# First attention of a four-stage block on one core: query items of one head by 512 tokens, values for two groups at once, masks written into the score bank, one block with its opening

## The chip, the cores and the metric

One NeuronCore of a Trainium2 chip runs the whole program. The metric is device time in microseconds (us) of one execution. TensorE (PE) multiplies, VectorE (DVE), ScalarE (ACT) and GpSimd (POOL) do everything between, SyncE's queue (SP) issues transfers.

## What is computed

`x` has 8 sequences of 128 tokens with 512 features. Four stages follow each other, each `x = x + tanh(gate) * stage(layernorm(x))`. Only the first changes:

```python
q = (query @ Wq).reshape(nb, q_len, H, D).transpose(0, 2, 1, 3)      # 32 heads of 128
k = (key @ Wk).reshape(nb, q_len, KVH, D).transpose(0, 2, 1, 3)      # 8 key heads
v = (value @ Wv).reshape(nb, q_len, KVH, D).transpose(0, 2, 1, 3)
q = q * cos + _rotate_half(q) * sin
k = k * cos + _rotate_half(k) * sin
k = jnp.repeat(k, GROUPS, axis=1)                                    # 4 query heads share a key head
v = jnp.repeat(v, GROUPS, axis=1)
scores = jnp.einsum('bhqd,bhkd->bhqk', q, k) / jnp.sqrt(jnp.float32(D))
scores = jnp.where(mask == 0, jnp.float32(-1000000000.0), scores)
attn = jax.nn.softmax(scores, axis=-1)
x = jnp.einsum('bhqk,bhkd->bhqd', attn, v)
return x.transpose(0, 2, 1, 3).reshape(nb, q_len, H * D) @ Wo
```

Keys and values come from `ctx`, queries from the normalised `x`. After it come a dequantised feed-forward, a second attention and a mixture of experts, which the change leaves as they are.

## The kernel before

Every large product is done in three fp32r parts: `product` (lines 119 to 124) multiplies the held operand's high part by the streaming operand's high part (L122) and low part (L123), and its low part by the streaming high part (L124). So each operand needs a copy to fp32r by ACT (`_hi`) and a subtraction by DVE or POOL (`_lo`).

**Opening** (its own `nc.Block`, lines 197 to 300). SP loads positions, gates, `x` in two halves, weights of group 0, the turned context and the mask. DVE makes layernorm statistics and normalises; PE turns the eight tiles (`norm_turn`, L116); ACT and DVE make `xT_hi` and `xT_lo` (L108, L98). POOL issues eight gathers of rotary rows (L219) first of all its work and then subtracts weights; PE turns the rotary rows (L293); ACT copies the context to `cT_hi` (L251), DVE and POOL each make two of the four `cT_lo`. At the end PE projects two items (`FIRST_ON_PE`).

**Attention** (a second block). Eight groups `g`, one key head and four query heads each. A group has eight units `u`, one sequence each, and ten items, each a 128x512 result in a bank: an item goes PE `project`, DVE `item_products` (one product with cos, L516, two with sin, L519), POOL `item_sum` (L410; for keys L406 and a scaling L408). A query item is two heads by 256 tokens: 24 products of 256 columns (`project_queries`, L170). A key item is 12 products of 512 columns. `place_of` says where an item goes; items 10 and up belong to the next group.

A unit goes through PE `score` (L634), DVE `keep_scores` (four `copy_predicated` of the open scores from the bank into `filled`, L528, and a maximum over `filled`, L531), ACT `exps` (L454), DVE `invert`, POOL `normalise` (L414), PE `turn_probs` (L641), ACT `probs_upper` (L461), DVE `probs_rest` (L539), PE `attend` (3 products), ACT `out_upper`, DVE `out_rest`, PE `project_out` (12 products), DVE `add_out` (L548).

The order of each engine is written out by hand: in step `s` of a group PE does `score(s)`, the step's items, in steps 0 and 1 half of the values, then `attend(s-2)`, `project_out(s-3)`, `turn_probs(s-1)`. So units run in a pipeline four steps deep. The values of a group are made turned (weights held, context streaming, two halves of 12 products), copied by ACT (`keep_values`), turned by PE (`turn_values`, L624), then split.

Weights of the next group are prepared inside the group: ACT does `queries_upper` in steps 4 and 5, `keys_values_upper` at the end of step 3, behind `probs_upper` of the step, and `out_weights` (four copies, L448) at the end of step 2. POOL follows with `wk_lo` (L152), `wv_lo`, `wq_lo`, `wo_lo` (L397). Items by step:

```python
ITEMS_OF_STEP = [[5], [6], [7], [8], [9], [10], [11], [12, 13, 14]]
FIRST_ITEMS = [0, 1, 2, 3, 4]
```

Items 2 and 3 (12 and 13 for the next group) are the key items, so keys of the next group are first needed in step 7. `score` of an even unit waits for the item sums that it reads (`rope_sum`).

## Time and profile before

| | us |
|---|---|
| median of 3 timed runs | 943.28 (940.91 to 947.6) |
| the profiled execution's own time | 939.19 |
| its span, first to last instruction | 937.3 |
| mean granted TensorE clock | 0.965 |
| busy: PE, PE weight loads, DVE, ACT, POOL | 849.8, 732.2, 665.1, 407.6, 427.7 |

The profile is one execution. Its page gives busy time by engine, 40 slices of the span, the chain of work that ended last, and the costliest groups of instructions. The trace behind it gives each instruction's start and duration (us from the span's start). A product's printed duration contains its fill and drain, which overlap with its neighbours: what a product costs in a stream is the distance from its start to the next start.

### The profile page before, as it was taken

How to read it: one execution, taken by the hardware profiler on the slowest of the kernel's cores; microseconds unless marked ns; L12 is line 12 of the kernel's file. 1: busy time of each engine (PE TensorE's matmuls, PEld its weight loads, DVE VectorE, ACT ScalarE, POOL GpSimd, SP SyncE). 2: the span in 40 equal slices, each digit the busy share in tenths (PEclk: the TensorE clock that was granted, in tenths of full speed). 3: DMA queues.
4: the chain of work that ended last, by engine and by line, in shares of the span. 5: the costliest groups of instructions: out<-in, count | busy, mean ns of one | idle time of the engine just before them, and what ended most of it. 6: DMA issues, size and time to landing. Idle time of an engine off the chain costs nothing. (4 is left out here: it accounts for less than half of the span.)

```text
span 937.3 us, 14384 instructions
## 1 busy us (share of the span) xinstructions
PE 849.8 (91%) x4952; PEld 732.2 (78%) x4952; DVE 665.1 (71%) x1332; ACT 407.6 (43%) x1001; POOL 427.7 (46%) x341
## 2 busy tenths in 40 slices
PE   2799999999999999999999999987899887999990
PEld 1788889889889888988988988865778665777770
DVE  5767758767767767766776776747582677999874
ACT  3335235335324424424424433435313425978870
POOL 6548417436435534633642732506300007877830
PEclk9999999999999999999999999998999967999995
DMA  8201101101101100200300200007100545999817
GB/s 345 84 1 45 68 2 46 68 0 45 67 0 45 67 0 7 105 0 0 112 0 0 90 1 1 1 1 287 45 5 8 224 180 177 348 339 346 324 40 270
DMA packets 23048, 88.88 MB, mean 95 GB/s; under 512 B 6512, under 2 KB 7024, under 8 KB 15200
## 3 DMA queue, kind: packets, MB, share of 16 engines
q1 hardware_dynamic: 16864, 78.90, 22.8%
q0 software_dynamic: 6144, 9.46, 2.9%
q8 instruction: 23, 0.38, 0.2%
q14 instruction: 17, 0.14, 0.0%
HBM read 85.18 MB, written 13.63 MB: 105 GB/s over the span
## 5 line engine op out<-in xcount | busy, mean ns | idle before, releaser
L410 POOL TENSOR_TENSOR qT<-straight,turned 128x512 f32<-128x512 f32 x64 | 82.5, 1288 | 239.6 <-DVE turned L519 239.6
L454 ACT ACTIVATE probs<-filled,negmax 128x128 f32<-128x128 f32 x256 | 99.7, 391 | 126.9 <-DVE negmax L531 126.9
L122 PE MATMUL bank<-xT_hi,wq_hi 128*128 128x256 f32 x512 | 149.3, 292 | 0.0
L124 PE MATMUL bank<-xT_hi,wq_lo 128*128 128x256 f32 x512 | 144.7, 283 | 0.0
L123 PE MATMUL bank<-xT_lo,wq_hi 128*128 128x256 f32 x512 | 144.6, 282 | 0.0
L519 DVE TENSOR_TENSOR turned<-bank,sinT 64x512 f32<-64x512 f32 x160 | 110.1, 688 | 2.2
L122 PE MATMUL bank<-wo_hi,oT_hi 128*128 128x512 f32 x256 | 102.4, 400 | 5.3 <-DVE oT_lo L543 4.2
L124 PE MATMUL bank<-wo_hi,oT_lo 128*128 128x512 f32 x256 | 100.1, 391 | 0.0
L123 PE MATMUL bank<-wo_lo,oT_hi 128*128 128x512 f32 x256 | 99.9, 390 | 0.0
L122 PEld LDWEIGHTS bank<-xT_hi,wq_hi 128*128 128x128 f32 x512 | 97.1, 190 | 0.4
L123 PEld LDWEIGHTS bank<-xT_lo,wq_hi 128*128 128x128 f32 x512 | 97.0, 189 | 0.3
L516 DVE TENSOR_TENSOR straight<-bank,cosT 128x512 f32<-128x512 f32 x80 | 55.3, 691 | 58.4 <-PE bank L124 57.0
L124 PEld LDWEIGHTS bank<-xT_hi,wq_lo 128*128 128x128 f32 x512 | 96.7, 189 | 0.0
L461 ACT ACTIVATE pT_hi<-bank 128x512 fp32r<-128x512 f32 x64 | 38.1, 595 | 115.1 <-PE bank L641 115.1
L548 DVE SCALAR_TENSOR_TENSOR x<-bank,gates,x 128x512 f32<-128x512 f32 x64 | 47.9, 748 | 36.8 <-PE bank L124 36.8
L1345 DVE TENSOR_TENSOR cT_lo<-ring,cT_hi 128x1024 fp32r<-128x1024 f32 x56 | 68.1, 1221 | 7.9 <-ACT cT_hi L1058 7.9
L414 POOL TENSOR_TENSOR probs<-probs,invtotal 128x512 f32<-128x512 f32 x64 | 66.6, 1041 | 12.7 <-DVE invtotal L535 12.7
L634 PE MATMUL bank<-kT,qT 128*128 128x128 f32 x512 | 67.6, 275 | 0.0
L122 PE MATMUL bank<-cT_hi,xT_hi 128*128 128x512 f32 x144 | 60.8, 422 | 5.6 <-DVE xT_lo L1339 5.5
L543 DVE TENSOR_TENSOR oT_lo<-bank,oT_hi 128x512 fp32r<-128x512 f32 x64 | 44.2, 691 | 29.2 <-ACT oT_hi L466 28.1
L122 PEld LDWEIGHTS bank<-wo_hi,oT_hi 128*128 128x128 f32 x256 | 48.0, 188 | 19.7 <-DVE oT_lo L543 5.4
L634 PEld LDWEIGHTS bank<-kT,qT 128*128 128x128 f32 x512 | 62.3, 192 | 0.1
(218 smaller groups left out, 2051.3 us busy)
## 6 DMA issues: line engine op xcount, KB each, us to landing
ring<-in_ew SPq DMA_DIRECT2D x28, 1024.0 KB, 6.9
raw_big<-in_wq SPq DMA_DIRECT2D x8, 1024.0 KB
raw_big<-in_wo SPq DMA_DIRECT2D x8, 1024.0 KB
early_w<-in_ew SPq DMA_DIRECT2D x8, 1024.0 KB
ring<-picked SPq DMA_DIRECT2D x8, 512.0 KB, 7.1
x<-in_x SPq DMA_DIRECT2D x2, 1024.0 KB
raw_k<-in_wk SPq DMA_DIRECT2D x8, 256.0 KB
raw_v<-in_wv SPq DMA_DIRECT2D x8, 256.0 KB
```

Of the source, the lines that this page charges most:

```text
L122: nc.tensor.matmul(out_, hi, r_hi, start=start, stop=False)
L123: nc.tensor.matmul(out_, hi, r_lo, start=False, stop=False)
L124: return nc.tensor.matmul(out_, lo, r_hi, start=False, stop=stop)
L410: nc.gpsimd.tensor_tensor(dst, shaped(straight[:, k, :], key), shaped(turned[:, k, :], key), ALU.add).then_inc(rope_sum, 1)
L414: nc.gpsimd.tensor_tensor(probs[:, u % 2, :, :], probs[:, u % 2, :, :], invtotal[:, u % UNITS, :].unsqueeze(2).broadcast_to([P, GR, S]), A ...
L454: ex = nc.scalar.activation(probs[:, u % 2, h, :], filled[:, u % UNITS, h, :], ACT.Exp, bias=negmax[:, u % UNITS, h:h + 1], accum_out=tota ...
L516: nc.vector.tensor_tensor(shaped(straight[:, k, :], key), shaped(bank[:, :], key), spread_over(cosT[:, tok], key), ALU.mult)
L519: last = nc.vector.tensor_tensor(shaped(turned[dst, k, :], key), shaped(bank[src, :], key), spread_over(sinT[src, tok], key), ALU.mult)
L543: nc.vector.tensor_tensor(oT_lo[:, u % 2, :, :], bank_o[:, :].rearrange("p (h t) -> p h t", h=GR), oT_hi[:, u % 2, :, :].bitcast(F32), ALU ...
L548: nc.vector.scalar_tensor_tensor(x[:, u % UNITS, :], bank_y[:, :], gates[:, 0:1], x[:, u % UNITS, :], ALU.mult, ALU.add).then_inc(y_added, 1)
L634: mm = nc.tensor.matmul(bank_scores[u % 2][:, h * S:(h + 1) * S], qT[:, (u // 2) % 2, h, q], kT[:, keys], start=True, stop=True)
L1345: nc.vector.tensor_tensor(expert_lo(k)[:, rows, :], ring[k % RING][:, rows, :], expert_hi(k)[:, rows, :].bitcast(F32), ALU.subtract).then_ ...
```

## The change

- Both blocks become one, `filled` and `vT` go, and the opening's buffers lie over attention buffers that are used later (`over`). The layernorm buffer has four tiles.
- A query item is one head by 512 tokens: 12 products of 512 columns. Items are reordered: 0 is keys of the first 512 tokens, 1 to 4 are heads for them, 5 keys of the rest, 6 to 9 heads for them. Steps 3 and 7 hold two items, all others one. `score` waits for sums at units 0 and 4 alone.
- Values are made unturned (context held, weights of two groups streaming, 256 columns): four fills of 24 products for a pair of groups. Groups 0 and 1 are filled in the opening; groups 2, 4 and 6 fill for themselves and the next in steps 0, 1, 2 and 4. `keep_values` and `turn_values` go.
- `keep_scores` writes -1e9 into the score bank where a key is closed; the maximum and the exponentials read the bank; `score(u)` waits for the exponentials of unit `u-2`.
- Weight copies and remainders for queries are done by head (four of 512 columns), for keys at the end of step 3, for values only in odd groups (steps 3 and 6).
- Opening: POOL does the key remainder before its gathers, and two value remainders between the fifth and the sixth gather; DVE makes all four `cT_lo`; ACT interleaves tiles 4 to 7 with the four context copies and does the value copies behind them; PE turns half of the rotary rows, makes item 0, turns the other half, then values and items 1 to 4 in turns.

The core of the diff:

```diff
+        def ln_bank(n, t):
+            return psum[t % 2 if n else 4 + t % 2]
...
+            ctx_raw = over("wo_hi", "ctx_raw", [P, KC, T])
+            xn = over("qT", "xn0", [P, 4, E], skip=4 * GR * HALF)
+            rotary = over("pT_hi", "rotary", [P, NB, 2 * D])
+            mask_raw = over("oT_hi", "mask_raw", [P, NB, S], I32)
+            raw_v1 = over("oT_lo", "raw_v1", [P, KC, D])
...
+            ITEMS_OF_STEP = [[5], [6], [7], [8, 9], [10], [11], [12], [13, 14]]
+            FIRST_ITEMS = [0, 1, 2, 3, 4]
+            KEY_ITEMS = (0, 5)
+            FILLS = NB // 2
+            FILL_OF_STEP = {0: 0, 1: 1, 2: 2, 4: 3}
...
+            def fills(g, odd):
+                return not odd and (not isinstance(g, int) or 0 < g < KVH)
+            def place_of(item):
+                i = item % ITEMS
+                if i in KEY_ITEMS:
+                    half = KEY_ITEMS.index(i)
+                    tok = slice(half * HALF, (half + 1) * HALF)
+                    return kT[:, tok], tok, True
+                half, h = (0, i - 1) if i < 5 else (1, i - 6)
+                return qT[:, half, h, :], slice(half * HALF, (half + 1) * HALF), False
+            def head_of(item):
+                return (item % ITEMS - 1) % 5
...
+                    load_out(0)
                     sp.dma_start(loaded[:, :, :], a["wk1"]).then_inc(g_in[0], 16)
-                    sp.wait_ge(wq_lo_s, 2)
-                    sp.dma_start(raw_big[:, :], a["wo"][0]).then_inc(big_in, 16)
+                    with sp.Fori(1, KVH - 2, 2) as g:
+                        load_keys(g)
+                        load_queries(g)
+                        load_out(g)
+                        load_values(g + 1)
+                        load_keys(g + 1)
+                        load_queries(g + 1)
+                        load_values(g + 2)
+                        load_out(g + 1)
+                    load_keys(KVH - 1)
+                    load_queries(KVH - 1)
+                    load_out(KVH - 1)
...
+                    def keys_rest(g):
+                        wait(pool, wk_hi_s, g, 1, 1)
+                        nc.gpsimd.tensor_tensor(wk_lo[:, :, :], raw_k[:, :, :], wk_hi[:, :, :].bitcast(F32), ALU.subtract).then_inc(wk_lo_s, 1)
+                    def values_weight_rest(g, half, raw):
+                        cols = slice(half * D, (half + 1) * D)
+                        wait(pool, wv_hi_s, g, 1, 1)
+                        nc.gpsimd.tensor_tensor(wv_lo[:, :, cols], raw[:, :, :], wv_hi[:, :, cols].bitcast(F32), ALU.subtract).then_inc(wv_lo_s, 1)
...
+                    def group(g, odd):
+                        for step, u, items, _, _, _ in steps(g):
+                            if step in (4, 5) and more(g):
+                                queries_rest(g + 1, 2 * (step - 4))
+                                queries_rest(g + 1, 2 * (step - 4) + 1)
+                            if u is not None and not items:
+                                normalise(g, u)
+                            for item in items:
+                                item_sum(g, item)
+                                if item == items[0]:
+                                    normalise(g, u)
+                            if step == 2 and u is not None:
+                                out_weights(g)
+                            if step == 3 and more(g):
+                                keys_rest(g + 1)
+                                if odd:
+                                    values_weight_rest(g + 1, 0, raw_v)
+                            if step == 6 and more(g) and odd:
+                                values_weight_rest(g + 2, 1, raw_v)
+                    nc.gpsimd.memset(masked[:, :], MASKED)
                     nc.gpsimd.memset(key_scale[:, :], float(D) ** -0.5)
+                    keys_rest(0)
                     pool.wait_ge(pos_step, 3)
                     for t in TILES:
                         pool.indirect_dma_start(
                             out=rotary[:, t, :], out_offset=None, in_=a["rotary"],
                             in_offset=bass.IndirectOffsetOnAxis(ap=pos_row[:, t:t + 1], axis=0)).then_inc(in_rot, 16)
-                    keys_values_rest(pool, 0)
-                    queries_rest(pool, 0, 0)
-                    queries_rest(pool, 0, 1)
-                    for c in (1, 3):
-                        pool.wait_ge(ctx_hi, c + 1)
-                        nc.gpsimd.tensor_tensor(cT_lo[:, c, :], ctx_raw[:, c, :], cT_hi[:, c, :].bitcast(F32),
-                                                ALU.subtract)
+                        if t == 4:
+                            values_weight_rest(0, 0, raw_v)
+                            values_weight_rest(1, 1, raw_v1)
+                    for h in range(GR):
+                        queries_rest(0, h)
+                    for item in FIRST_ITEMS:
+                        item_sum(0, item)
+                    group(0, False)
+                    with pool.Fori(1, KVH - 2, 2) as g:
+                        group(g, True)
+                        group(g + 1, False)
+                    group(KVH - 1, True)
+                    group(KVH, False)
...
+                    def keys_upper(g):
+                        wait(act, k_in, g, 16, 16)
+                        wait(act, proj_mm, g, ITEMS, 6 - ITEMS)
+                        nc.scalar.activation(wk_hi[:, :, :], raw_k[:, :, :], ACT.Copy).then_inc(wk_hi_s, 1)
...
+                    def exps(g, u):
+                        wait(act, score_max, g, UNITS, u + 1)
+                        wait(act, pT_mm, g, UNITS, u - 1)
+                        for h in range(GR):
+                            ex = nc.scalar.activation(probs[:, u % 2, h, :], bank_scores[u % 2][:, h * S:(h + 1) * S], ACT.Exp,
+                                                      bias=negmax[:, u % UNITS, h:h + 1], accum_out=total[:, u % UNITS, h:h + 1])
...
+                    def group(g, odd):
+                        for step, u, items, turn, attend, _ in steps(g):
+                            if step in (4, 5) and more(g):
+                                if step == 4:
+                                    wait(act, proj_mm, g, ITEMS, 10)
+                                queries_upper(g + 1, 2 * (step - 4))
+                                queries_upper(g + 1, 2 * (step - 4) + 1)
+                            if u is not None:
+                                exps(g, u)
+                            if attend is not None:
+                                out_upper(g, attend)
+                            if step in FILL_OF_STEP and fills(g, odd):
+                                values_upper(g, FILL_OF_STEP[step])
+                            if turn is not None:
+                                probs_upper(g, turn)
+                            if step == 2 and u is not None:
+                                out_weights(g)
+                            if step == 3 and more(g):
+                                keys_upper(g + 1)
+                                if odd:
+                                    wait(act, v_mm, g, 2, 2)
...
                     nc.scalar.activation(gates[:, :], gates_raw[:, :], ACT.Tanh)
                     norm_sqrt(act, 0, HALVES[0])
-                    norm_upper(act, 0, 0)
-                    norm_upper(act, 0, 1)
-                    keys_values_upper(act, 0)
-                    norm_upper(act, 0, 2)
-                    norm_upper(act, 0, 3)
+                    for t in HALVES[0]:
+                        norm_upper(act, 0, t)
+                    keys_upper(0)
                     norm_sqrt(act, 1, HALVES[1])
-                    queries_upper(act, 0, 0)
-                    queries_upper(act, 0, 1)
-                    for t in HALVES[1]:
-                        norm_upper(act, 0, t)
                     for c in range(KC):
-                        act.wait_ge(in_ctx[c // 2], 16)
+                        norm_upper(act, 0, 4 + c)
+                        act.wait_ge(in_ctx[c], 16)
                         nc.scalar.activation(cT_hi[:, c, :], ctx_raw[:, c, :], ACT.Copy).then_inc(ctx_hi, 1)
-                    keep_cos(0)
-                    keep_cos(1)
+                    act.wait_ge(v_in, 32)
+                    values_weight_upper(0, 0, raw_v)
+                    values_weight_upper(1, 1, raw_v1)
+                    keep_rotary(0)
+                    for h in range(GR):
+                        queries_upper(0, h)
+                    keep_rotary(1)
+                    for f in range(FILLS):
+                        values_upper(0, f)
+                    act.wait_ge(ctx_lo, KC)
+                    group(0, False)
...
+                    def keep_scores(g, u):
+                        wait(dve, score_mm, g, UNITS, u + 1)
+                        nc.vector.memset(gatepost[:, :], 0.0)
+                        for h in range(GR):
+                            kept_ = nc.vector.copy_predicated(bank_scores[u % 2][:, h * S:(h + 1) * S], closed_key[:, u, :],
+                                                              masked[:, :].broadcast_to([P, S]))
+                        kept_.then_inc(score_kept, 1)
+                        wait(dve, score_kept, g, UNITS, u + 1)
+                        nc.vector.tensor_reduce(negmax[:, u, :], bank_scores[u % 2][:, :].rearrange("p (h k) -> p h k", h=GR),
+                                                AX.X, ALU.max, negate=True).then_inc(score_max, 1)
...
+                            if step in FILL_OF_STEP and fills(g, odd):
+                                values_rest(g, FILL_OF_STEP[step])
...
+                    def make_values(g, f):
+                        wait(pe, wv_lo_s, g, 1, 2)
+                        wait(pe, v_lo_s, g, 2, f)
+                        for j in range(2):
+                            tok = slice((2 * f + j) * S, (2 * f + j + 1) * S)
                             for c in range(KC):
-                                mm = product(bank[:, :], wk_hi[:, c, :], wk_lo[:, c, :], cT_hi[:, c, tok], cT_lo[:, c, tok], c == 0, c == KC - 1)
-                        else:
-                            mm = project_queries(j, bank, tok)
-                        mm.then_inc(proj_mm, 1)
...
                     def score(g, u):
-                        if u % 2 == 0:
-                            wait(pe, rope_sum, g, ITEMS, 4 + u if u else 3)
-                        wait(pe, score_kept, g, UNITS, u - 1)
+                        if u % 4 == 0:
+                            wait(pe, rope_sum, g, ITEMS, 5 + 5 * (u // 4))
+                        wait(pe, exp_done, g, UNITS, u - 1)
                         keys = slice(u * S, (u + 1) * S)
-                        q = slice((u % 2) * S, (u % 2 + 1) * S)
+                        q = slice((u % 4) * S, (u % 4 + 1) * S)
                         for h in range(GR):
-                            mm = nc.tensor.matmul(bank_scores[u % 2][:, h * S:(h + 1) * S], qT[:, (u // 2) % 2, h, q], kT[:, keys], start=True, stop=True)
...
+                    def attend(g, odd, u):
+                        own = odd if u >= 0 else not odd
+                        if not own and u % 2 == 0:
+                            wait(pe, v_lo_s, g, 2, u // 2 + 1)
                         wait(pe, pT_lo_s, g, UNITS, u + 1)
                         wait(pe, o_lo_s, g, UNITS, u)
-                        product(bank_o[:, :], v_hi[:, u % UNITS, :], v_lo[:, u % UNITS, :], pT_hi[:, u % 2, :], pT_lo[:, u % 2, :], True, True).then_inc(o_mm, 1)
+                        cols = slice(D, 2 * D) if own else slice(0, D)
+                        product(bank_o[:, :], v_hi[:, u % UNITS, cols], v_lo[:, u % UNITS, cols], pT_hi[:, u % 2, :], pT_lo[:, u % 2, :], True, True).then_inc(o_mm, 1)
...
+                    turn_rotary(0)
+                    pe.wait_ge(wk_lo_s, 1)
+                    for c in range(KC):
+                        pe.wait_ge(ctx_lo, c + 1)
+                        mm = product(bank_rope[0][:, :], wk_hi[:, c, :], wk_lo[:, c, :], cT_hi[:, c, 0:HALF], cT_lo[:, c, 0:HALF], c == 0, c == KC - 1)
+                    mm.then_inc(proj_mm, 1)
+                    turn_rotary(1)
+                    make_values(0, 0)
+                    pe.wait_ge(ln_lo, NB)
+                    for item in FIRST_ITEMS[1:]:
+                        project(0, item)
+                        if item < FILLS:
+                            make_values(0, item)
+                    group(0, False)
+                    with pe.Fori(1, KVH - 2, 2) as g:
+                        group(g, True)
+                        group(g + 1, False)
```

## Rows read from the trace of the kernel before

**Rows 1.** Windows: length; busy of PE, PEld, DVE, ACT, POOL; PEclk; DMA; GB/s
```profile
190.18:263.51 73.33, 73.33 (x466) 65.36 (x465) 52.34 (x113) 29.54 (x92) 35.18 (x28) 1.00 0.10 36
49.08:116.85 67.77, 64.56 (x420) 56.93 (x419) 48.88 (x108) 26.92 (x88) 38.20 (x31) 1.00 0.11 40
782.60:786.60 4.00, 4.00 (x10) 3.15 (x11) 2.33 (x3) 2.65 (x4) 3.13 (x3) 0.50 0.37 129
```
**Rows 2.** Timeline of PE: scores that open steps of a group, start and us
```profile
200.59 1.06 PE L634 MATMUL bank<-kT,qT 128*128 128x128 f32 x8
...
212.14 1.06 PE L634 MATMUL bank<-kT,qT 128*128 128x128 f32 x8
...
219.75 1.06 PE L634 MATMUL bank<-kT,qT 128*128 128x128 f32 x8
...
227.49 1.06 PE L634 MATMUL bank<-kT,qT 128*128 128x128 f32 x8
```
**Rows 3.** Timeline of PE in step 7: where pieces of work begin
```profile
253.98 0.40 PE L122 MATMUL bank<-cT_hi,wk_hi 128*128 128x512 f32 x1
...
256.77 0.28 PE L122 MATMUL bank<-xT_hi,wq_hi 128*128 128x256 f32 x1
...
259.63 0.40 PE L122 MATMUL bank<-pT_hi,v_hi 128*128 128x512 f32 x1
260.33 0.39 PE L122 MATMUL bank<-wo_hi,oT_hi 128*128 128x512 f32 x1
...
263.08 0.60 PE L641 MATMUL bank<-ident,probs 128*128 128x128 f32 x4
263.51 1.06 PE L634 MATMUL bank<-kT,qT 128*128 128x128 f32 x8
```
**Rows 4.** Timeline of ACT, then POOL, behind step 3
```profile
227.69 0.60 ACT L461 ACTIVATE pT_hi<-bank 128x512 fp32r<-128x512 f32 x1 [2.70 <-PE bank L641]
228.18 0.62 ACT L163 ACTIVATE wk_hi<-raw_k 128x512 fp32r<-128x512 f32 x1
...
229.40 1.29 POOL L152 TENSOR_TENSOR wk_lo<-raw_k,wk_hi 128x512 fp32r<-128x512 f32 x1 [0.97 <-ACT wv_hi L164]
```
**Rows 5.** Timeline of the opening
```profile
13.91 0.95 POOL L219 DMA_INDIRECT rotary<-in_rotary,pos_row  x1 [0.30 <-issue]
...
16.70 0.60 ACT L108 ACTIVATE xT_hi<-bank 128x512 fp32r<-128x512 f32 x1 [0.46 <-PE bank L116]
...
23.12 0.60 ACT L108 ACTIVATE xT_hi<-bank 128x512 fp32r<-128x512 f32 x1
...
28.34 3.62 PE L293 MATMUL bank<-ident,rotary 128*128 128x128 f32 x16
...
29.08 1.05 ACT L251 ACTIVATE cT_hi<-ctx_raw 128x1024 fp32r<-128x1024 f32 x1
...
40.59 0.47 PE L122 MATMUL bank<-cT_hi,wk_hi 128*128 128x512 f32 x1 [2.56 <-DVE turned L519]
```
**Rows 6.** Timeline: a gather of rows and the transpose that waits for it
```profile
774.99 1.16 POOL L963 DMA_INDIRECT words<-xn_rows,place_token  x1 [4.75 <-DVE place_token L1276]
...
778.45 1.11 PE L1551 MATMUL bank<-ident,words 128*128 128x128 f32 x4 [4.58 <-DMA words<-xn_rows,place_token]
```
**Rows 7.** Timeline of DVE and POOL in step 3: item product, sum, normalising
```profile
223.69 0.69 DVE L516 TENSOR_TENSOR straight<-bank,cosT 128x512 f32<-128x512 f32 x1 [0.88 <-PE bank L124]
224.40 1.39 DVE L519 TENSOR_TENSOR turned<-bank,sinT 64x512 f32<-64x512 f32 x2
...
226.14 1.28 POOL L410 TENSOR_TENSOR qT<-straight,turned 128x512 f32<-128x512 f32 x1
227.38 1.04 POOL L414 TENSOR_TENSOR probs<-probs,invtotal 128x512 f32<-128x512 f32 x1
```
**Rows 8.** Groups of instructions by line: the masking copies; busy us, mean ns
```profile
L528 DVE COPY_PREDICATED filled<-open_key,bank 128x128 f32<-128x128 int8 x256 | 57.1, 298 | 0.0
```
**Rows 9.** Timeline of SP's queue: the first transfer behind the attention
```profile
632.89 0.34 SPq L843 DMA_DIRECT2D words<-in_wint  x1
```

642 lines of the change are left out of this document (257 added, 385 removed).

## The prediction, made before the run

> **What bounds the kernel now.** I read the window table first. It shows one middle group of the first attention: 73.33 us long, PE busy for 73.33 of them, at the full granted clock (1.00), while DVE has 52.3, POOL 35.2 and ACT 29.5 [rows 1]. Groups 1 to 6 are alike. So from the second group on, each microsecond taken from PE's own sequence is one microsecond of the kernel, and what the others save is worth nothing until PE waits for them. Then I read PE's timeline by the starts of the scores, which open the steps. Steps 0, 1, 2 and 3 take 200.59 - 190.18 = 10.41, 11.55, 7.61 and 7.74 us [rows 1, 2]. Last the timelines of ACT and POOL around step 3 and of the opening [rows 4, 5], since the change moves waits there. The stages behind the attention (their first transfer starts at 632.89 [rows 9]) are unchanged and start later or earlier with its end.
>
> **Prices in a stream.** They are distances between starts at the full clock. Twelve products of 512 columns: 256.77 - 253.98 = 2.79 us (0.2325 each). Twenty-four of 256: 259.63 - 256.77 = 2.86 (0.119 each). Attending 0.70, projecting out 2.75, four transposes 0.43 [rows 3]. A plain step is 7.61, and with a 512-wide item 7.54.
>
> **Term 1, query items.** All 64 become 12 products of 512: 64 x 0.07 = -4.5 us. The nearest row is the key item with the same shape; the products with `wo` run a little closer (2.75 for twelve), which would give 64 x 0.11 = 7.0. I take 4.5, since the key items, too, stream a wide context tile.
> The Trainium skill (TensorE: Matmul & The Clock Gate, "Wait — 56ns, not 53.3ns?") puts N columns at N / 2.4 GHz plus some 2.5 ns. The trace disagrees: these rows lie 10 to 17 ns above it. By that rule the item would go from 2.62 to 2.59 us, 64 x 0.03 = 2 us in all, and the sum would end 2.5 us higher.
>
> **Term 2, values.** Step 0 costs 10.41 - 7.61 = 2.80 and step 1 costs 3.94 more than a plain step; that is the whole of making, copying and turning them, with its small waits: 8 x 6.74 = 53.9 us. The change makes 16 fills of 24 products of 256 columns (4 in the opening, 12 in groups 2, 4, 6): 16 x 2.86 = 45.8. Their copies and remainders are as many as before, and PE waits for none: a fill's copy has a step's time. -8.1 us.
>
> **Term 3, step 3.** It is 0.13 us longer than a plain one before, as PE waits there for `wo_lo`. With two items in this step the wait goes: 8 x 0.13 = -1.0. The second item is moved, not added.
>
> **Term 4, the keys' weights.** This speaks against the change. ACT's `keys_upper(g+1)` stays at the end of step 3, behind `probs_upper(2)`, which needs the transposes that PE does last in step 3. Before, the keys were first multiplied in step 7, four steps later, and this was free. Now item 10, the first thing behind `score(4)` in step 4, is a key item. Let T be the start of `score(4)`; in the rows T is 227.49. ACT starts `pT_hi` at T + 0.20 and `wk_hi` at T + 0.69, done at T + 1.31 [rows 4]. POOL follows some 0.08 later (before it waited for `wv_hi` as well), takes 1.29 (T + 2.68), and PE starts after another hand-over of 0.1: T + 2.8. `score(4)` frees PE at T + 0.81. So PE waits 2.0 us, with `attend(2)`, `project_out(1)` and `turn_probs(3)` queued behind item 10. It happens in groups 0 to 6: 7 x 2.0 = +14.0. Bounds: nothing, if some other engine were late anyway; 7 x 2.8, if ACT or POOL are 0.8 later. The chain has no other cover.
>
> **Term 5, the start of PE's run.** Now POOL issues its gathers first; the last starts at 13.91 and the rows are long there when PE turns them at 28.34 [rows 5]. After, POOL does `keys_rest(0)` first, and ACT makes `wk_hi` only behind tile 3 (copy at 16.70, so `wk_hi` to 17.4, `wk_lo` to 18.8). Five gathers at 0.95 + 0.30 = 1.25 end at 25.1. Then POOL waits for `wv_hi`. ACT reaches it behind tiles 4 to 7 and four context copies: from 22.7 (tile 4, 0.4 earlier than its 23.12, since four buffers spare a wait) four times some 0.5 and four times 1.0, and about 0.3 of waiting: 28.9. First value copy to 29.5, two remainders of 1.3 on POOL to 32.2, three gathers, the last starting at 34.7. A gather's rows are read 778.45 - 774.99 = 3.46 after its start [rows 6]: 38.1. PE's `turn_rotary(0)` stands there, in front of everything else: 38.1 against 28.34, +9.7. The 16 transposes take about 3.3 before (3.62 with the last one's drain), all slow; then eight slow and eight fast, 2.6: -0.7. And item 0 runs half in the slow state, as the first products did before: 512-wide products in a stretch granted 0.50 take some 0.4 against 0.23 [rows 1]; six by 0.2, less 0.4 before, +0.8. Sum +9.8. Bounds: 5 less, if ACT reaches `wv_hi` as soon as its weights could be there; 3 more for its alternation with DVE, which now makes all `cT_lo`.
>
> **Term 6, waits before the first score.** Before, PE stood 2.56 us at 40.59, between the blocks [rows 5]. Now `score(0)` waits for the sum of item 4, the item just projected: 0.2, then DVE 2.1 (0.69 + 1.39), POOL 1.28 and two hand-overs [rows 7], 3.7 us. +1.1. The first score starts at about 71 instead of 49.08 (11.4 of that are the four fills of term 2).
>
> **Term 7, group 0.** From the group of 73.33, without three projections out, two attendings and one turning (3 x 2.75 + 2 x 0.70 + 0.43 = 10.1), group 0 should take 63.2, and takes 67.77 [rows 1]: 4.5 of waits for copied values and late `wo_lo`. After, with nothing but items between the scores, `turn_probs(0)` comes too early: DVE's item 5 ends at 6.0 from the first score, POOL's two key operations at 8.4, normalising at 9.5, PE would be there at 7.3: 2.2. And `wo_lo` and two sums behind it let `score(4)` wait 1.9, which overlaps the key wait but for 0.4. So 2.6: -1.9.
>
> **Free:** masks in the bank (DVE, four of 298 ns before [rows 8], and 0.88 us idle before an item's product [rows 7]), exponentials, `filled`, `vT`, loads. `score(4)` and the next `score(0)` now wait for the sum of an item projected in the same step: PE needs 0.70 + 2.75 + 0.43 = 3.88 after it, DVE and POOL 0.2 + 2.1 + 1.3 + 0.1 = 3.7. A margin of 0.2, so free, but only just.
>
> **Sum.** -4.5 - 8.1 - 1.0 + 14.0 + 9.8 + 1.1 - 1.9 = +9.4 us. Against the profiled execution's 939.19 (span 937.3) that is 948.6. That execution was 4.1 under the median of the runs, 943.28, and on that median the sum gives 952.7. I say 953. Some 1% (9.4 us) is about what a measurement tells from no change.
>
> **Rivals.**
> - *Sums late.* The margin of 0.2 is gone (a DVE or POOL operation 0.2 to 0.7 later), and PE waits in steps 4 and 0 of each group: 15 x 0.5 = 7.5, 960. For: nothing covers it. Against: both chains are measured.
> - *Masks dear.* A masking copy in the bank, reading a broadcast value, costs double: DVE has 1.2 us more per step, its 6.4 (52.3 less two value remainders of 0.69, over eight steps) becomes 7.6 of 7.54. With 0.3 us per step by 64, 972. No row shows such a copy. Against: DVE's other operations take 0.69 us from bank or memory alike.
> - *Opening shorter.* POOL gets `wv_hi` early, -5: 948.
> - *Keys' wait covered.* -14: 939. For it PE would have to be late in step 3 for another reason; rows 1 show none.
> - *The other side: wide products near the stream limit.* Faster by 1% takes 19 us off the forecast, 0.30 per query item, so under 0.208 us a product. 512 columns at 2.4 GHz are 0.213; the twelve measured take 0.2325. If they overlapped to 0.13, 64 x 1.2 = 77 less, 875. The Trainium skill's same page ("Back-to-back issue gap") gives about 131 ns for 512 columns in pairs with weight loads, which would be this case; the rows disagree with it everywhere.
>
> **How the numbers follow.** Forecast 0.52 (948 to 958, split at 952.7 about half: 0.27 slower, 0.25 same). Sums late 0.14 and masks dear 0.07: slower. Opening shorter 0.11: same. Keys' wait covered 0.13, of which 0.02 under 934: same, faster. Wide products 0.03: faster. Together slower 0.48, same 0.47, faster 0.05. The range 940 to 963 leaves out the dear masks, the wide products and half of the covered wait, 0.17.
>
> **What would show it.** PE's timeline: one idle piece of 2.0 us per group in front of a key item behind `score(4)`, released by POOL's `wk_lo`; first score near 71; pairs of groups of 147.3 (67.9 and 79.4) against 146.7; no idle in front of the scores. The first transfer behind the attention starts near 642 instead of 632.89. I am wrong if the gathers end before 33, if item 10 starts right behind the score, or if DVE is busy near 100%.

## The result and the profile after

| | before | after |
|---|---|---|
| median of 8 timed runs each, us | 943.61 (938.08 to 947.6) | 954.8 (948.68 to 958.58) |
| ratio to before, 95% interval | | 1.013 (1.010 to 1.016) |
| the profiled execution's own time | 939.19 | 953.25 |
| its span | 937.3 | 951.4 |
| first score of the attention starts at | 49.08 | 70.84 |
| first transfer behind the attention | 632.89 | 647.17 |

The kernel is 1.3% slower. 953 was forecast, with 940 to 963 as its range. All of it lies ahead of the first transfer behind the attention, which starts 14.28 us later in the two profiled executions; by the ratio of all runs the change costs 12.3 us. What follows that transfer takes 304.2 us (951.4 - 647.17), and took 304.4 before.

The window table of the changed kernel: group 0, group 1 (odd, no values made), group 2 (even, with the four fills that make the values of two groups). They answer [rows 1].

```profile
core 0: us, PE busy (x) PEld busy (x) DVE busy (x) ACT busy (x) POOL busy (x), PEclk, DMA share, GB/s
70.84:134.53 63.69, 60.08 (x290) 49.70 (x291) 47.48 (x103) 24.99 (x86) 34.18 (x29) 0.95 0.12 42
134.53:202.68 68.15, 66.42 (x339) 55.46 (x337) 53.01 (x111) 26.81 (x91) 36.83 (x31) 1.00 0.11 40
202.68:282.14 79.46, 77.73 (x434) 66.70 (x433) 55.38 (x115) 28.06 (x93) 34.29 (x29) 1.00 0.10 34
```

A pair is 68.15 + 79.46 = 147.61 us long, where two groups took 146.66 before. PE is no longer busy throughout: 1.73 us of each group are idle. The list of PE's waits names them (us in all, times, longest):

```profile
engine line waited for: us in total, times, longest us
PE bank L120 <- DVE xn L96: 23.1, 4, 11.4
PE bank L672 <- DMA rotary<-in_rotary,pos_row: 11.6, 1, 11.6
PE bank L126 <- POOL wk_lo L297: 10.4, 6, 1.7
...
PE bank L620 <- POOL qT L326: 5.1, 2, 3.5
```

Four lines, four readings. L120 is the turning of tiles in the opening, as before. L672, the turning of the rotary rows, waits 11.6 us for the gathers (the address-driven loads of these rows that POOL issues). L126, the first product of a key item, waits 1.7 us for `wk_lo` in six groups; PE takes up work slowly after it, so a step with the wait is 2.0 us longer (9.56 against 7.56). L620 is `score`: two waits, both in group 0, and none in any later group.

PE's timeline through the opening and group 0 (start and us, with the idle time before it in brackets), which answers [rows 5]:

```profile
38.71 1.97 PE L672 MATMUL bank<-ident,rotary 128*128 128x128 f32 x8 [11.57 <-DMA rotary<-in_rotary,pos_row]
...
70.84 1.16 PE L620 MATMUL bank<-kT,qT 128*128 128x128 f32 x8 [3.53 <-POOL qT L326]
76.19 1.05 PE L620 MATMUL bank<-kT,qT 128*128 128x128 f32 x8
82.03 0.66 PE L627 MATMUL bank<-ident,probs 128*128 128x128 f32 x4 [1.98 <-POOL probs L330]
82.52 1.88 PE L620 MATMUL bank<-kT,qT 128*128 128x128 f32 x8
88.50 0.60 PE L627 MATMUL bank<-ident,probs 128*128 128x128 f32 x4
88.93 1.06 PE L620 MATMUL bank<-kT,qT 128*128 128x128 f32 x8
...
101.03 1.16 PE L620 MATMUL bank<-kT,qT 128*128 128x128 f32 x8 [1.57 <-POOL qT L326]
109.04 1.06 PE L620 MATMUL bank<-kT,qT 128*128 128x128 f32 x8
```

Step 0 lasts 76.19 - 70.84 = 5.35 us, step 2 88.93 - 82.52 = 6.41 and step 4 109.04 - 101.03 = 8.01. The windows over steps 0, 1 and 2 show what is odd in the first and the third:

```profile
70.84:76.19 5.35, 5.35 (x21) 4.40 (x22) 1.86 (x6) 2.12 (x6) 0.00 (x0) 0.68 0.02 3
76.19:82.52 6.33, 4.35 (x26) 3.45 (x24) 5.98 (x14) 2.18 (x12) 3.33 (x3) 1.00 0.00 0
82.52:88.93 6.41, 6.41 (x29) 5.49 (x28) 3.55 (x10) 2.34 (x10) 2.27 (x2) 0.73 0.01 1
```

PE never idles in them, yet the granted clock is 0.68 and 0.73: part of each ran at the lower of the two levels. I call such a stretch a dip. The prediction has none in group 0.

### The profile page after: what moved, and what is told of

It is laid out like the page before. It is cut to its first block and busy times, and to the rows that moved or that the text cites. A ratio compares the mean times of both kernels' runs of the same rounds, so it can differ in the third digit from the quotient of the medians.

```text
span 951.4 us, 13052 instructions
## 1 busy us (share of the span) xinstructions
PE 841.3 (88%) x4312; PEld 698.9 (73%) x4312; DVE 675.3 (71%) x1332; ACT 391.6 (41%) x1003; POOL 421.4 (44%) x355
## 3 DMA queue, kind: packets, MB, share of 16 engines
q1 hardware_dynamic: 17152, 78.90, 22.6%
## 5 line engine op out<-in xcount | busy, mean ns | idle before, releaser
L403 ACT ACTIVATE probs<-bank,negmax 128x128 f32<-128x128 f32 x256 | 90.7, 367 | 133.9 <-DVE negmax L502 133.9
L126 PE MATMUL bank<-xT_hi,wq_hi 128*128 128x512 f32 x256 | 106.1, 415 | 0.0
L126 PE MATMUL bank<-wo_hi,oT_hi 128*128 128x512 f32 x256 | 100.4, 392 | 4.7 <-DVE oT_lo L515 4.7
L128 PE MATMUL bank<-xT_hi,wq_lo 128*128 128x512 f32 x256 | 101.1, 395 | 0.0
L127 PE MATMUL bank<-xT_lo,wq_hi 128*128 128x512 f32 x256 | 100.7, 393 | 0.0
L415 ACT ACTIVATE oT_hi<-bank 128x512 fp32r<-128x512 f32 x64 | 38.7, 605 | 89.1 <-PE bank L128 89.1
L620 PE MATMUL bank<-kT,qT 128*128 128x128 f32 x512 | 68.8, 278 | 5.1 <-POOL qT L326 5.1
L498 DVE COPY_PREDICATED_SCALAR bank<-closed_key,masked 128x128 f32 x256 | 71.1, 346 | 1.8 <-issue 1.8
L620 PEld LDWEIGHTS bank<-kT,qT 128*128 128x128 f32 x512 | 63.0, 193 | 5.9 <-POOL qT L326 5.8
L126 PE MATMUL bank<-cT_hi,xT_hi 128*128 128x512 f32 x144 | 61.2, 425 | 5.3 <-DVE xT_lo L1335 5.0
L126 PEld LDWEIGHTS bank<-wo_hi,oT_hi 128*128 128x128 f32 x256 | 48.1, 188 | 16.6 <-DVE oT_lo L515 6.2
L967 POOL DMA_INDIRECT picked<-loaded,place_row x36 | 45.2, 1255 | 33.0 <-ACT loaded L1060 19.1
```

The source lines that it names most:

```text
L126: nc.tensor.matmul(out_, hi, r_hi, start=start, stop=False)
L127: nc.tensor.matmul(out_, hi, r_lo, start=False, stop=False)
L128: return nc.tensor.matmul(out_, lo, r_hi, start=False, stop=stop)
L403: ex = nc.scalar.activation(probs[:, u % 2, h, :], bank_scores[u % 2][:, h * S:(h + 1) * S], ACT.Exp, bias=negmax[:, u % UNITS, h:h + 1], ...
L498: kept_ = nc.vector.copy_predicated(bank_scores[u % 2][:, h * S:(h + 1) * S], closed_key[:, u, :], masked[:, :].broadcast_to([P, S]))
L620: mm = nc.tensor.matmul(bank_scores[u % 2][:, h * S:(h + 1) * S], qT[:, u // 4, h, q], kT[:, keys], start=True, stop=True)
```

## The experiments

All are timed beside the kernel before, whose median moved between 940.1 and 943.6 from one set of runs to the next; so I compare ratios. 1% is 9.4 us. Line numbers shift by one or so between the kernels; the names don't.

| kernel | median, us | ratio to before (95%) | first score at | group 1 starts at | first transfer behind |
|---|---|---|---|---|---|
| the change | 954.80 | 1.013 (1.010 to 1.016) | 70.84 | 134.53 | 647.17 |
| keys' weights early | 940.22 | 0.9987 (0.997 to 1.0005) | 72.16 | 133.69 | 634.39 |
| gathers first | 944.33 | 1.0034 (1.0005 to 1.0062) | 60.30 | 122.38 | 635.14 |
| fills one item later | 947.89 | 1.007 (1.0043 to 1.0097) | 68.34 | 130.43 | 643.41 |
| all three | 923.92 | 0.9829 (0.9798 to 0.986) | 56.83 | 117.04 | 617.76 |
| query items in halves | 959.63 | 1.0156 (1.0126 to 1.0186) | 72.70 | 137.86 | 655.45 |
| spare products | 951.14 | 1.008 (1.0052 to 1.0108) | 71.05 | 133.13 | 646.10 |
| ScalarE's rounding alone early | 947.35 | 1.004 (1.0016 to 1.0063) | 71.98 | 136.94 | 640.06 |
| the kernel before with masks in the bank | 942.25 | 0.9995 (0.9972 to 1.0017) | | | 634.45 |
| fills made twice | 999.58 | 1.0621 (1.0579 to 1.0662) | 82.08 | 144.20 | 691.65 |
| all three, one fill in step 0 | 925.42 | 0.9824 (0.9792 to 0.9856) | 54.27 | 117.25 | 617.82 |

### The keys' weights, prepared two steps earlier

```diff
-                            if step == 3 and more(g):
+                            if step == 1 and more(g):
                                 keys_upper(g + 1)        # ACT; the same for keys_rest(g + 1) on POOL
```

(shortened: the value weights of odd groups, which followed in the same branch, stay at the end of step 3)

> The changed kernel with one thing moved: ACT's copy and POOL's remainder of the next group's key weights at the end of step 1 instead of step 3. Theory (the keys' weights are late for item 10): the idle piece of 2.0 us in front of each group's key item behind score(4) goes, seven times, span 951.4 - 14.0 = 937.4 us, pairs of groups 143.6 instead of 147.6 us, ratio to the kernel before about 0.998. Rival (sums late: something else holds PE in step 4, so the wait is only covered): another wait of up to 2 us shows in front of score(4) or the key item, and the span stays above 945.

Measured: 0.9987, so 1.4% (13.5 us) below the change. PE's waits hold no line for `wk_lo` any more, and a group is full again. Its windows over groups 1 and 2:

```profile
133.69:199.86 66.17, 66.17 (x339) 55.38 (x337) 53.01 (x111) 26.73 (x91) 36.95 (x31) 1.00 0.12 41
199.86:277.34 77.48, 77.48 (x435) 66.64 (x433) 55.42 (x115) 28.21 (x93) 34.42 (x29) 1.00 0.10 35
```

Both groups are 1.98 us shorter than the change's (66.17 against 68.15, 77.48 against 79.46), and PE is busy for all of them. Term 4 is right in place and size. The first score stood 1.3 us later in this execution (72.16 against 70.84), mostly because some nine products of item 0 ran slow and not three; the edit doesn't touch that stretch.

### ScalarE's part of it alone

```diff
+                            if step == 3 and more(g):
+                                keys_upper(g + 1)
                             if turn is not None:
                                 probs_upper(g, turn)
...
                             if step == 3 and more(g):
-                                keys_upper(g + 1)
```

> The changed kernel, with only ScalarE's rounding of the next group's key weights (wk_hi) moved ahead of the rounding of pT in step 3; GpSimd's remainder stays where it is. In the changed kernel [rows 4 show the same chain in the kernel before] wk_hi starts behind pT_hi and the remainder ends 1.7 us after PE wants it. Theory: wk_hi comes a rounding of pT earlier (0.5 us) or more, if ScalarE stood idle before pT was ready, so the wait of PE in step 4 falls from 2.0 us to somewhere between 0.1 and 1.5 us, in 7 groups: 3 to 13 us off, 942 to 951 us, most likely 945. The rival: GpSimd's queue, not ScalarE's, holds the remainder back (the normalising of the probabilities and four sums stand ahead of it), and then the time stays within 1.5 us of 954.8.

Measured: 1.004, 0.9% (8.5 us) below the change. From group 1 to the first transfer it takes 640.06 - 136.94 = 503.12 us, the change 512.64, keys' weights early 500.70. So most of the six waits go (9.5 of 11.9 us) with ACT's place in the queue alone. What held the chain was mainly ACT doing `pT_hi` first, as [rows 4] show it. With both moved two steps earlier another 2.4 us go, 0.4 a group; POOL's queue can hold back no more than that. PE's scores of steps 4, 5 and 6 in group 1:

```profile
170.06 1.06 PE L621 MATMUL bank<-kT,qT 128*128 128x128 f32 x8
...
177.99 1.06 PE L621 MATMUL bank<-kT,qT 128*128 128x128 f32 x8
...
185.56 1.06 PE L621 MATMUL bank<-kT,qT 128*128 128x128 f32 x8
```

Step 4 is 7.93 us, step 5 7.57; in the change step 4 is 9.57.

### The gathers first

```diff
-                    keys_rest(0)
                     pool.wait_ge(pos_step, 3)
                     for t in TILES:
                         pool.indirect_dma_start(...)
-                        if t == 4:
-                            values_weight_rest(0, 0, raw_v)
-                            values_weight_rest(1, 1, raw_v1)
+                    keys_rest(0)
+                    values_weight_rest(0, 0, raw_v)
+                    values_weight_rest(1, 1, raw_v1)
```

> The changed kernel with POOL's order in the opening undone: eight gathers first, then the key and the two value remainders. Theory (the gathers hold PE's whole run): rotary rows are turned right behind tile 7 near 28; fills begin when POOL has both value remainders, near 33.4 instead of 44.57, and the first score comes near 59.6 instead of 70.84; span 951.4 - 11.2 = 940.2, ratio about 1.001. Rival (ACT and DVE, which alternate on tiles 4 to 7 and the context, or POOL's value remainders hold PE as much): the first score comes at 65 or later, span 945 or more.

Measured: 1.0034, 1.0% (9.1 us) below the change, with the first score at 60.30, 10.54 earlier. POOL's timeline of it:

```profile
3.34 1.11 POOL L357 DMA_INDIRECT rotary<-in_rotary,pos_row  x1 [2.47 <-DVE pos_row L553]
...
12.34 1.06 POOL L357 DMA_INDIRECT rotary<-in_rotary,pos_row  x1 [0.30 <-issue]
17.83 1.26 POOL L297 TENSOR_TENSOR wk_lo<-raw_k,wk_hi 128x512 fp32r<-128x512 f32 x1 [4.43 <-ACT wk_hi L379]
29.87 4.04 POOL L302 TENSOR_TENSOR wv_lo<-raw_v,wv_hi 128x512 fp32r<-128x512 f32 x2 [10.78 <-ACT wv_hi L384]
```

The change's own POOL timeline, its key remainder and its last gather:

```profile
17.21 1.26 POOL L297 TENSOR_TENSOR wk_lo<-raw_k,wk_hi 128x512 fp32r<-128x512 f32 x1 [16.34 <-ACT wk_hi L380]
...
35.96 0.95 POOL L358 DMA_INDIRECT rotary<-in_rotary,pos_row  x1 [0.30 <-issue]
```

The eight gathers end at 13.4 instead of 36.9. The first remainder starts at 17.83 against 17.21, but the gathers don't cost it that: in the kernel with all three moves, which has the same order, it starts at 17.21 again. In this execution `x` came in later, and DVE's statistics of it began at 7.92 instead of 7.31. So the order of POOL's queue alone gives back what term 5 had put at 9.8.

### The opening's fills one item later

```diff
                     for item in FIRST_ITEMS[1:]:
                         project(0, item)
-                        if item < FILLS:
-                            make_values(0, item)
+                        if item > 1:
+                            make_values(0, item - 1)
```

(PE's part; DVE's `values_rest` is put an item later in the same way)

> The changed kernel with the fills of the opening one item later, so that the last fill (2.86 us) stands between item 4 and the first score. Theory (the 3.5 us of waiting lower the clock for the work behind it): the wait before score(0) shrinks to about 0.8, which gives 2.7, and step 0 of group 0 takes 3.7 instead of 5.35 us, another 1.7; span near 947, 945.5 if the slow stretch near 83 goes too. Rival (the slow stretch has nothing to do with the wait): step 0 still takes 5.35 us, span 948.7.

Measured: 1.007, 0.6% (5.7 us) below the change. The last fill now stands between item 4 and `score(0)`, whose wait falls from 3.53 to 0.72 us, and the first score starts 2.5 us earlier. Steps 0 to 2 took 3.80, 6.33 and 4.83 us at clock 1.00; step 4 took 9.56 instead of 8.01, so that a part of the gain was lost again:

```profile
68.34:72.14 3.80, 3.80 (x21) 3.25 (x22) 2.44 (x7) 0.68 (x1) 0.00 (x0) 1.00 0.02 4
72.14:78.47 6.33, 4.34 (x25) 3.45 (x24) 5.98 (x14) 3.62 (x17) 3.33 (x3) 1.00 0.00 0
78.47:83.30 4.83, 4.83 (x29) 4.11 (x28) 3.48 (x10) 2.11 (x10) 2.27 (x2) 1.00 0.01 2
```

### Spare products in the wait

```diff
+                    for c in range(KC):
+                        product(bank_y[:, :], wq_hi[:, c, 0:D], wq_lo[:, c, 0:D], xT_hi[:, c, 0:HALF], xT_lo[:, c, 0:HALF], c == 0, c == KC - 1)
                     group(0, False)
```

> The changed kernel, with 12 spare products of 256 columns ahead of score(0) of group 0; they write a bank that nothing reads before it is written anew, so the output doesn't hang on them. They fill 1.4 to 1.7 us of PE's 3.53 us wait for the sum of item 1, which stays what releases score(0). If the half-level clock in step 0 came from that wait, the first score still starts at 70.8 us, step 0 takes about 3.8 us instead of 5.35, and the span is 1.5 to 3 us shorter than the changed kernel's (949.5 us, 953 as a median). The rival: the clock falls for another cause, step 0 stays at 5.3 us, and the time stays at 954.8.

Two things in this expectation are not as the kernel has them. The wait is for the sum of item 4, and `HALF` is 512 tokens, so the twelve products have 512 columns and not 256: they fill 2.79 us, and the wait falls from 3.53 to 0.74 us.

Measured: 1.008, 0.5% (4.7 us, give or take 4) below the change. The span is 949.4 as expected, and the first score starts 0.2 us later than in the change; this kernel does more work and is no slower, by the runs even faster. In the traces the gain is less than in the ratios: the first transfer behind the attention comes 1.1 us earlier. The clock's dips are gone from steps 0 and 2, but not from group 0:

```profile
71.05 1.16 PE L620 MATMUL bank<-kT,qT 128*128 128x128 f32 x8 [0.74 <-POOL qT L326]
74.85 1.05 PE L620 MATMUL bank<-kT,qT 128*128 128x128 f32 x8
81.18 1.06 PE L620 MATMUL bank<-kT,qT 128*128 128x128 f32 x8
86.02 1.06 PE L620 MATMUL bank<-kT,qT 128*128 128x128 f32 x8
98.09 1.16 PE L620 MATMUL bank<-kT,qT 128*128 128x128 f32 x8 [1.54 <-POOL qT L326]
107.64 1.06 PE L620 MATMUL bank<-kT,qT 128*128 128x128 f32 x8
```

Step 0 is 3.80 instead of 5.35 and step 2 4.84 instead of 6.41, together 3.1 us less; but step 4 is 9.55 instead of 8.01, 1.5 more. There products of 512 columns start 0.43 us apart instead of 0.23. Group 0 takes 62.08 us, 1.6 less than in the change, and the later groups and the first score give 0.5 of it back.

Read over all ten kernels with this attention, by the lengths of the steps:

| kernel | wait before the first score | dip in step 0 | in step 2 | in step 4 |
|---|---|---|---|---|
| the change; halves; ScalarE's rounding early | 3.53 | yes | yes | no |
| keys' weights early; fills twice | 3.5 | yes | no | no |
| gathers first | 3.53 | no | no | yes |
| fills one item later; spare products | 0.7 | no | no | yes |
| all three | 0.7 | no | no | no |
| all three, one fill in step 0 | 0.7 | no | no | yes |

Five of the six with the long wait had the dip in step 0, none of the four with the short one; the sixth (gathers first) had the wait and no dip there. So the long wait goes with a dip but isn't all of the rule, and a dip taken away in one place can come up in another. A dip costs 1.3 to 1.6 us; in step 0 of two kernels (halves, ScalarE's rounding early) it lasted longer (clock 0.54 over the step instead of 0.68) and cost 2.7 and 2.8. No dip follows the 1.7 us waits for `wk_lo` in the later groups. Each line of the table rests on one execution of its kernels. Item 0 is the same work in the change and in keys' weights early, and three of its products ran slow in the one and nine in the other; so chance between executions isn't ruled out.

### Query items in halves again

```diff
+                            for k in range(2):
+                                part = slice(tok.start + 256 * k, tok.start + 256 * (k + 1))
+                                for c in range(KC):
+                                    mm = product(bank[:, 256 * k:256 * (k + 1)], ..., xT_hi[:, c, part], xT_lo[:, c, part], ...)
```

> The changed kernel, with each query item's products as two halves of 256 columns again (24 products of 256 columns where there were 12 of 512; the same bank, the same order of the items). The theory, from the rows [rows 2] and the trace of the changed kernel, has a query item 0.07 us dearer in halves: PE's pairs of groups 147.6 + 8 x 0.07 = 148.2 us long, the whole 64 x 0.07 = 4.5 us longer than the changed kernel, 959.3 us beside a kernel before of 943.6 (ratio 1.0166). The rival: how the columns are cut costs nothing here (954.8, 1.012). A second rival, that the wide products saved far more than 0.07 each item, would show as step 7 of a group well over 7.6 us.

Measured: 1.0156, 0.3% above the change (2.5 us). The theory had 1.0166, the rival 1.012, which is just outside the interval, but the change's own 1.013 is no more exact than that. The time alone hardly tells; the trace does. Two scores one plain step apart:

```profile
119.71 1.06 PE L626 MATMUL bank<-kT,qT 128*128 128x128 f32 x8
127.35 1.06 PE L626 MATMUL bank<-kT,qT 128*128 128x128 f32 x8
```

A step of 7.64 against 7.56, group 1 68.74 against 68.15: 0.59 / 8 = 0.074 us an item, 4.7 us over 64. Term 1 had 0.07. The first transfer behind the attention comes 8.3 us later than in the change, though. Beyond the items, 1.6 us of this lie in the opening and 0.9 in group 0, where more products ran at the lower clock level, and some 0.5 in the last step of group 2 and of group 4.

### The fills made twice

```diff
-                        for j in range(2):
+                        for j in (0, 1, 0, 1):
```

> The changed kernel with each of the 16 fills of values made twice over (48 products of 256 columns in place of 24, the second pass writing the same numbers again), to price a fill by itself. In the trace of the changed kernel a fill takes 24 x 0.119 = 2.85 us. If PE sets the end in each step that has a fill, the time grows by 16 x 2.85 = 45.6 us, to 1000.4 us (ratio to before 1.060), and a pair of groups grows from 147.6 to 159.0 us. The rival: part of the fills lies beside waits of PE (for the keys' weights, for the sums in group 0), so that it costs less than its own time: under 43 us. A second rival: values made in wide products crowd another engine or a bank, and it costs more than 48 us.

Measured: 1.0621, 4.9% above the change: 46.3 us for 16 fills, 2.9 each, against 45.6 expected. Group 2 grows from 79.46 to 91.41 us:

```profile
212.34:303.75 91.41, 89.27 (x530) 78.07 (x529) 55.93 (x115) 28.38 (x94) 34.30 (x29) 1.00 0.08 30
```

PE has 96 products more (530 against 434) and is busy for 11.5 us more, DVE for 0.6. By the scores, the four steps with a fill grow by 2.89, 2.80, 2.81 and 2.89, which makes 11.4; the other 0.6 is in the last step, where the loop turns. A fill lies bare on PE, so the price in term 2 is the whole price.

### The masks alone, in the kernel before

```diff
-                            kept = nc.vector.copy_predicated(filled[:, u, h, :], open_key[:, u, :], bank_scores[u % 2][:, h * S:(h + 1) * S])
+                            kept = nc.vector.copy_predicated(bank_scores[u % 2][:, h * S:(h + 1) * S], closed_key[:, u, :],
+                                                             masked[:, :].broadcast_to([P, S]))
```

(shortened: the maximum and the exponentials read the bank as well, and a score waits for `exp_done`)

> The kernel before, with the masks alone changed as in the change: masked entries are written into the score's own bank, the maximum is taken from there and the exponential reads the bank; the score that uses a bank again waits for the exponential of two units before instead of the masking. Theory: nothing of this ends on PE's path; the banks are free long before, so the time is that of the kernel before within 1 us (943.6, ratio 1.000). The rival (masks dear): scores wait for the exponentials in each step, 0.3 us or more in 64 steps, 963 us or more (ratio 1.02), and a row of waits of the scores on ScalarE appears.

Measured: 0.9995 (0.9972 to 1.0017): no change clear of the noise. No score waits for an exponential in PE's list of waits. In the trace the first transfer behind the attention starts at 634.45 instead of 632.89, and a middle group takes 73.5 us instead of 73.33. So the masks cost 1.6 us at the most, where the rival had 19. The groups by line show why there is something to hide at all; 31 units of the changed kernel, which answer [rows 8]:

```profile
L403 ACT ACTIVATE probs<-bank,negmax 128x128 f32<-128x128 f32 x124 | 44.0, 367 | 62.5 <-DVE negmax L502 62.5
L498 DVE COPY_PREDICATED_SCALAR bank<-closed_key,masked 128x128 f32 x124 | 34.4, 346 | 0.0
```

A masking copy takes 346 ns (in the experiment too) where it took 298: 4 x 0.05 = 0.2 us a step for DVE, which idles 0.9 us and more in each. The rival had 1.2.

### All three together

The three edits of keys, gathers and fills in one kernel.

> The three moves together. Theory (the three losses lie one behind the other on PE and add up): 14.0 + 11.2 + 4.4 = 29.6 less, span 921.8, ratio 0.981 or a little above. Rival (they overlap or another engine becomes the bound once PE is not held): span above 930.

Measured: 0.9829 (0.9798 to 0.986), 1.7% faster than the kernel before and 3.0% below the change. The three alone gave 1.43 + 0.96 + 0.60 = 2.99%, so they add up. The first score starts at 56.83 and group 0 takes 60.21 us, without a dip. This is the version to keep.

### One fill of the opening in step 0

```diff
+                            if isinstance(g, int) and g == 0 and step == 0:
+                                make_values(0, FILLS - 1)
```

(the same place in ACT's and DVE's orders; the opening makes the other two an item later again)

> The version with all three moves (key weights at the end of step 1, gathers first, the opening's fills one item later), and in it the last fill of the opening made in step 0 of group 0, behind its query item, the other two an item later again. There PE waited 1.99 us for the first probabilities before it turned them; the fill of 2.85 us would fill that. Theory: 2.0 us off its 923.9, so 921.9 us (ratio to before 0.981), with turn_probs(0) not waiting and no wait longer than 0.8 us before score(0). The rival: the opening's items then follow one another faster than their rotation and their weights, PE waits there for what it gains, and the time stays at 923.9.

Measured: 0.9824 (0.9792 to 0.9856), the same as without it: a miss. The wait of `turn_probs(0)` is gone and group 0 starts at 54.27, 2.56 earlier; group 1 starts at 117.25, 0.21 later. The loss is in steps 3 and 4. PE's timeline there, and the window behind that score, in this kernel:

```profile
82.52 1.77 PE L623 MATMUL bank<-kT,qT 128*128 128x128 f32 x8 [2.08 <-POOL qT L326]
```

```profile
82.52:86.52 4.00, 4.00 (x15) 3.47 (x16) 1.80 (x6) 1.47 (x4) 1.75 (x2) 0.57 0.21 86
```

The same window in the kernel with the three moves alone:

```profile
83.88:87.88 4.00, 4.00 (x21) 3.44 (x22) 1.80 (x7) 2.08 (x7) 1.80 (x2) 1.00 0.22 86
```

Of the 2.77 us, 0.6 went into a longer wait of `score(4)` for its sum (2.08 against 1.51), which a PE that comes earlier only waits out, and 1.6 into a dip behind it (15 products in 4 us instead of 21, step 4 9.24 instead of 7.67). The remaining 0.6 is the step that took the fill: 6.65 + 4.13 for steps 0 and 1, against 3.80 + 6.33 without it. My rival had named the wrong place.

## Why the prediction was right, point by point

- **What bounds.** PE's sequence: right. Doubling the fills moved the time by the fills' own length, and the 48 ns more of each masking copy moved the attention by 1.6 us at the most.
- **Term 1, query items, -4.5.** Right in size (0.074 an item against 0.07). The wide product takes 0.2325 us in the stream also here. The rule of the Trainium skill (TensorE: Matmul & The Clock Gate, "Wait — 56ns, not 53.3ns?"), N / 2.4 GHz plus some 2.5 ns, stays 17 ns below that for these fp32r products, and the gain was 4.7 us and not the 2 us that an estimate from it gives.
- **Term 2, values, -8.1.** Right. Group 2 is 79.46 - 68.15 = 11.31 longer than group 1, 2.83 a fill; 2.86 was taken.
- **Term 3, step 3, -1.0.** Right: step 3 with its two items is 10.36 us, a plain 7.56 and 2.80 for the second item, with nothing over.
- **Term 4, the keys' weights, +14.0.** Right, and the largest: 2.0 us in each of six groups. In group 0 it lay beside the wait of `score(4)` but for some 0.35 (step 4 took 8.01, and 7.66 with all three moves), as term 7 had it.
- **Term 5, the start of PE's run, +9.8.** Right in sum: the rotary rows were turned at 38.71, 38.1 was forecast; the gathers alone are worth 10.5 in the experiment. That it came out so near is luck in part, for errors inside it met. POOL's two value remainders took 3.97 us instead of 2.6, so the last gather started at 35.96 and not at 34.7; but its rows were read 2.75 us after its start, where [rows 6] had 3.46. And item 0 ran slow for three products only, not for half of it (for some nine of them in three other kernels).
- **Term 6, +1.1.** Right as a wait: 3.53, 3.7 was forecast.
- **Term 7, group 0, -1.9.** The one that was mis-sized. Its waits were right (1.98 and 1.57 against 2.2 and 1.9), but the group took 63.69 us where all terms together gave 67.77 - 1.9 + 2.0 - 6.74 - 0.56 - 0.13 = 60.4. The 3.2 us between are the two dips of the clock, in steps 0 and 2. The check is the version with all three moves: no dip, and 60.21 + 0.35 for the key wait that it doesn't have, 60.56. The forecast had no dip and gave no reason why there should be none.
- **The rest.** The three pairs took 147.6 each instead of 147.3, 1.0 in all. The last group, whose five items are its only ones, took 69.73 where 76.05 - 6.74 - 0.35 - 0.13 gives 68.8: 0.6 of the 0.9 between is that PE waited 5.8 us in it, behind the last items, instead of 5.2. With the first score 0.3 early that makes 3.2 + 1.0 + 0.9 - 0.3 = 4.8 over the sum of +9.4, against a measured 14.28 - 9.4 = 4.9. The ratio of all runs, 1.3%, is 12.3 us; it lies between. So 953 against 954.8 looks closer than the sum was: +9.4 stands against 12.3 by the ratio and 14.3 by the traces.
- **The rivals.** *Sums late*: `score` waits twice, both in group 0, and in no steady group; the margin of 0.2 held. *Masks dear*: the copies are dearer, by 48 ns and not by double, and all but hidden. *Opening shorter*: no, ACT reached `wv_hi` at about the time forecast (POOL begins behind it at 29.32, 29.5 was forecast). *Keys' wait covered*: only in group 0. *Wide products near the stream limit*: no.

The wait that the change added was foreseen because the queue was followed item by item: the first use of `wk_lo` moved from step 7 to step 4, its making didn't move.

## What to carry to other kernels

When work is reordered, list for each operand the step in which it is made and the step in which it is first used, on every engine's queue; here two such pairs that the change had brought together (key weights and item 10, gathers and the rotary turning) cost 22.6 us by the two experiments, and moving the producers ahead in their queues gave it back. A wait ahead of a busy stretch may cost more than its length, because what follows can run at the lower clock level: fill it with work that is needed anyway. And a wait that is filled only pays as far as the next fixed time on the path: the fill in step 0 gained 2.6 us and lost it again two waits later.

## What was not expected of the hardware

- The clock fell to its lower level (products of 512 columns 0.43 us apart instead of 0.23) in short stretches of group 0 that came with waits of 1.5 to 3.5 us, in nine of ten kernels (all but that with the three moves), and never behind the 1.7 us waits of the steady groups (clock 1.00 in all their windows). Which wait is followed by a dip isn't settled: the kernel with the gathers first had the 3.53 us wait and no dip behind it. Each kernel has one trace, so I can't say how often it falls elsewhere for the same kernel. The first products of item 0 vary too: three slow ones in the change, nine in the kernel with ScalarE's rounding early, whose first score comes 1.1 us later.
- Two remainders on POOL took 3.97 us (4.04 with the gathers first), where a single one takes 1.27 to 1.29 in a steady group. In that stretch DVE subtracts `cT_lo`. The timelines of POOL and DVE:

```profile
29.32 3.97 POOL L302 TENSOR_TENSOR wv_lo<-raw_v,wv_hi 128x512 fp32r<-128x512 f32 x2 [4.45 <-ACT wv_hi L385]
...
31.59 1.71 POOL L302 TENSOR_TENSOR wv_lo<-raw_v,wv_hi 128x512 fp32r<-128x512 f32 x1
```

```profile
29.29 1.22 DVE L566 TENSOR_TENSOR cT_lo<-ctx_raw,cT_hi 128x1024 fp32r<-128x1024 f32 x1
30.42 1.75 DVE L569 TENSOR_SCALAR closed_key<-mask_raw 128x1024 int8<-128x1024 int32 x1
```

  The pair's second row is the second remainder alone. The Trainium skill (SBUF — State Buffer, "Who interferes with whom") says that a DVE instruction with two inputs in SBUF contends with a GpSimd instruction that reads SBUF, over a port pair that is locked and not shared. The first remainder agrees: begun at the end of `cT_lo`, 30.51, a remainder of 1.28 would end at 31.79, and it ends at 31.62. The second doesn't follow from that: it runs when `cT_lo` is over, beside `closed_key`, and still takes 1.71 us, 0.43 more than alone. No run here took either away, so both are readings and not shown.
- A masking copy that writes the bank from a broadcast value takes 346 ns against 298 for one that writes SBUF from the bank; an exponential reads the bank in 367 ns against 391 from SBUF.
- What follows the attention, the same code in all kernels, took between 302.4 and 308.4 us in their profiled executions. Times of single executions say nothing about 3 us; the starts of the scores in the trace do.
